# Row-by-row fetches by SyncE for 37 tiles of a graph network's gathers

## The reference

```python
h = relu(layernorm(x)); x = x + L0(h, edges)   # mean over neighbours, [h, mean] @ W.T + b
h = relu(layernorm(x)); x = x + L1(h, src, dst)
#   theta = h[dst] - h[src]; w = sigmoid(relu(theta @ W1 + b1) @ W2 + b2)
#   segment_sum(w * theta, dst) + indeg * (h @ W4 + b4)
h = relu(layernorm(x)); x = x + L2(h, edges)   # relu(h @ Wp.T + bp)[src], mean by dst, elu, normalised
h = relu(layernorm(x)); x = x + L3(h, ...)
#   all_h[etype, src] * edge_weight, segment_sum by dst, + h @ loop_weight
```

## Time and profile before

| | |
|---|---|
| Time, median of three runs | 5245.48 us (5244.3 to 5245.74) |
| Time of the profiled execution | 5255.77 us |
| Its span, first to last instruction | 5253.4 us |
| Mean granted TensorE clock | 0.846 of full speed |
| Busy: PE, DVE, ACT, POOL | 73%, 56%, 30%, 70% of the span |
| Gathers at line 1535 | 790 in layers 1 and 3, 1563 in layer 2, 1203 in layer 4 |
| DMA queue of SP and its packets | 145692 packets, 288.54 MB |

### The profile page before, as it was taken

One profiled execution on the slowest core, in us unless ns is written; L12 is line 12 of the kernel. 1 busy time (PEld: TensorE's weight loads), 2 busy tenths in 40 slices (PEclk: granted clock), 3 DMA queues, 4 the chain that ended last, 5 costly groups with the idle time before them and its releaser, 6 DMA issues.

```text
span 5253.4 us, 75208 instructions
## 1 busy us (share of the span) xinstructions
PE 3851.4 (73%) x22393; PEld 2977.7 (57%) x22393; DVE 2942.4 (56%) x9882; ACT 1575.8 (30%) x5791; POOL 3668.8 (70%) x3899
## 2 busy tenths in 40 slices
PE   3889999665666556566665488879899999999544
PEld 3345555655565555555555455445677777777443
DVE  7998876665555566666666744444544433333232
ACT  5555443433333333333333401132112222221000
POOL 5345553677777777777777477757777777777776
PEclk7799999877777777877778799989999999998655
DMA  4234443555555555555555556556111111111222
GB/s 124 69 123 141 145 145 125 166 156 158 157 157 157 157 156 158 159 159 158 159 161 161 153 191 201 200 178 244 52 50 51 51 51 50 51 51 52 53 73 53
DMA packets 303264, 663.89 MB, mean 126 GB/s; under 512 B 70592, under 2 KB 152924, under 8 KB 293388
## 3 DMA queue, kind: packets, MB, share of 16 engines
q0 software_dynamic: 155152, 369.61, 25.7%
q1 hardware_dynamic: 145692, 288.54, 16.3%
q10 hardware_dynamic: 2016, 0.92, 0.1%
HBM read 545.40 MB, written 113.38 MB: 125 GB/s over the span
## 4 chain that ended last, share of the span: by engine, by line
POOL 48%; PE 21%; issue 17%; DVE 9%; DMA 2%; ACT 2%; DVEq 1%; SPq 0%; ACTq 0%; POOLq 0%
POOL rows L1535 40%; POOL third L1535 8%; PE ps L2721 6%; PE ps L2618 3%; PE ps L2706 3%; PE ps L2630 2%; PE ps L2679 2%; DVE tmp L2019 2%; PE ps L2567 1%; PE ps L2686 1%; DVE oneh L1928 1%; DVE turned_words L2020 1%; DVE rows L2020 1%; DMA rows<-tab_hp,idx_src 1%; ACT h L1710 1%
## 5 line engine op out<-in xcount | busy, mean ns | idle before, releaser
L1535 POOL DMA_INDIRECT rows<-tab_rel,third x1203 | 1190.4, 990 | 366.7 <-issue 364.0
L1535 POOL DMA_INDIRECT rows<-tab_hp,idx_src x1120 | 1083.5, 967 | 345.2 <-issue 335.9
L2744 PE MATMUL ps<-third 128*128 128x128 f32 x3126 | 626.4, 363 | 729.4 <-DVE third L2049 728.7
L1535 POOL DMA_INDIRECT rows<-tab_h,idx_src x790 | 772.2, 977 | 541.2 <-PE ps L2686 276.2
L2744 PEld LDWEIGHTS ps<-third 128*128 128x128 f32 x3126 | 548.3, 264 | 790.5 <-DVE third L2049 789.5
L1758 ACT ACTIVATE turned_words<-turned_words 128x128 f32<-128x128 f32 x1563 | 463.2, 297 | 1251.0 <-DVE turned_words L2062 1251.0
L2721 PE MATMUL ps<-third,h 128*128 128x385 bf16 (+1 forms) x3626 | 742.7, 335 | 44.3 <-DMA h<-cnt_d 24.6
L2679 PE MATMUL ps<-oneh,rows 128*128 128x128 f32 x2406 | 403.2, 320 | 262.8 <-DMA rows<-tab_rel,third 160.1
L2679 PEld LDWEIGHTS ps<-oneh,rows 128*128 128x128 f32 x2406 | 352.5, 225 | 330.3 <-issue 183.2
L1535 POOL DMA_INDIRECT third<-tab_hp,idx_src x443 | 426.9, 964 | 135.0 <-issue 133.8
L2721 PEld LDWEIGHTS ps<-third,h 128*128 128x128 bf16 x3626 | 351.5, 100 | 293.8 <-issue 29.6
(11 more groups left out here) (305 smaller groups left out, 5685.6 us busy)
## 6 DMA issues: line engine op xcount, KB each, us to landing
third<-dst_flat SPq DMA_DIRECT2D x390, 256.0 KB, 3.5
cnt_d<-h SPq DMA_DIRECT2D x37, 1568.0 KB, 5.8
h<-cnt_d SPq DMA_DIRECT2D x37, 1568.0 KB
tab_rel<-third SPq DMA_DIRECT2D x49, 512.0 KB, 3.1
rows<-tab_rel,third POOLq DMA_INDIRECT x1203, 2.5
rows<-tab_hp,idx_src POOLq DMA_INDIRECT x1120
rows<-tab_h,idx_src POOLq DMA_INDIRECT x790
third<-tab_hp,idx_src POOLq DMA_INDIRECT x443
```

Source lines behind the costliest of these rows:

```text
L1535: pool.indirect_dma_start(out=to[:, t, 0:n], out_offset=None, in_=table[:, :], in_offset=bass.IndirectOffsetOnAxis(ap=idx[:, col:col + 1], ...
L2744: last = pe.matmul(ps_t[sl][:, t * P:(t + 1) * P], onehT[:, sl, t * P:(t + 1) * P], pwin[:, st["v"] % 2, :], start=True, stop=True)
```

## The change

In layer 2 the last tile of groups 20, 40, ..., 380 (19 tiles) and in layer 4 the last tile of groups 108, 124, ..., 380 (18 tiles) is no longer gathered by POOL. In each of the 16 turns that end two turns before the group's own, SP loads eight indices from one partition into registers and issues eight DMAs, each of one row, from the table to one partition of a buffer; there are two buffers a layer, in parts of `third` and of `key` that lie unused. In the group's turn SP waits until all 128 rows are there and the group's slot is free, and copies the buffer to the slot's last tile with one DMA. DVE's `hidden` and PE's `scatter` wait for this copy too. The indices come, one partition a tile, by 19 DMAs of 128 words at the start of layer 2, for which SP waits, and by 18 DMAs of one column of `parked` (128 words that lie apart) ahead of the loads of `late`.

```diff
--- before.py
+++ after.py
@@ -29,6 +29,8 @@
 BUNDLE = 128
 SPARE_COLS = 8
 OFF_LOAD = 8
+SINGLES = {1: (("sp", 20, 20),), 3: (("sp", 18, 16),)}
+ROW_LOAD = 8
 
 PACKS3 = ((4, 36, 2), (2, 76, 2), (1, 148, 2), (1, 244, 3))
 SLOTS3, NQ3 = 16, 3
@@ -226,7 +228,8 @@
         cut.append(cut[3] + (HP_SLOT - HP_FIRST) * hp_words)
         hT_early = third[:, cut[4]:cut[4] + CH * P]
         stage2_early = third[:, cut[4] + CH * P:cut[4] + 2 * CH * P].rearrange("p (b f) -> p b f", f=P)
-        assert cut[4] + 2 * CH * P <= nb * H3 // 2
+        cut.append(cut[4] + 3 * CH * P)
+        assert cut[5] + 4 * P <= nb * H3 // 2
         rows_hp = [v.rearrange("p (t f) -> p t f", f=2 * P + 1) for v in hp_at]
         dst_bc = third[:, cut[0]:cut[1]].rearrange("p (s e) -> p s e", s=3)
         onehT = third[:, cut[1]:cut[2]].rearrange("p (s e) -> p s e", s=2)
@@ -272,6 +275,11 @@
         key = sb("key", [P, npt])
 
         key3 = key[:, 0:nth]
+        single_at = {(1, "sp"): [third[:, cut[5] + k * 2 * P:cut[5] + (k + 1) * 2 * P] for k in range(2)]}
+        for n, who in enumerate(("sp", "act")):
+            single_at[3, who] = [key[:, CH * P + (2 * n + k) * P:CH * P + (2 * n + k + 1) * P] for k in range(2)]
+        idx_single = {1: key[:, 2 * CH * P:2 * CH * P + P].bitcast(I32), 3: key[:, 2 * CH * P:2 * CH * P + P].bitcast(I32)}
+        assert nth <= CH * P
         rest0 = key[:, 0:2 * CH * P].rearrange("p (s b f) -> p s b f", s=2, f=P)
         wsum = sb("wsum", [BUNDLE, P + 2])
         gsum = sb("gsum", [P, P + 2])
@@ -370,6 +378,9 @@
         s_wlo = sem("s_wlo")
         s_place = sem("s_place")
         s_off = sem("s_off")
+        s_rowidx = sem("s_rowidx")
+        s_moved = {(layer, who): [sem(f"s_moved{layer}{who}{k}") for k in range(2)] for layer in SINGLES for who, _, _ in SINGLES[layer]}
+        s_single = {(layer, who): [sem(f"s_single{layer}{who}{k}") for k in range(2)] for layer in SINGLES for who, _, _ in SINGLES[layer]}
         s_key3 = sem("s_key3")
         s_key3T = sem("s_key3T")
         s_idx3 = sem("s_idx3")
@@ -849,13 +860,32 @@
                 n_scat.update(n_scat_head)
                 added_before = s_add.value
             n_bc, n_pw, n_oneT, n_expand, n_hid, n_z, n_gate = ({} for _ in range(7))
+            singles, single_of, single_full, n_moved = {}, {}, {}, {}
+            for who, first, step in SINGLES.get(layer, ()):
+                singles[who] = list(range(g0 + first, ng - ROW_LOAD, step))
+                single_of.update((g, (who, j)) for j, g in enumerate(singles[who]))
+
+            def single_rows(g):
+                for who in singles:
+                    for j, at in enumerate(singles[who]):
+                        r0 = (g - (at - P // ROW_LOAD - 1)) * ROW_LOAD
+                        if 0 <= r0 < P:
+                            if r0 == 0:
+                                single_full[who, j] = s_single[layer, who][j % 2].up(16 * P)
+                            free = n_moved[singles[who][j - 2]] if j > 1 and r0 == 0 else None
+                            plan.append(("single_rows", dict(layer=layer, who=who, j=j, r0=r0, free=free)))
 
             def gather(g):
                 if g in n_row:
                     return
                 sl = g % slots
-                n_row[g] = s_row[sl].up(16 * tiles[g])
-                plan.append(("gather", dict(layer=layer, g=g, slot=sl, free=slot_free.get(sl))))
+                n_row[g] = s_row[sl].up(16 * (tiles[g] - (g in single_of)))
+                plan.append(("gather", dict(layer=layer, g=g, slot=sl, free=slot_free.get(sl), n=tiles[g] - (g in single_of))))
+                if g in single_of:
+                    who, j = single_of[g]
+                    n_moved[g] = s_moved[layer, who][j % 2], s_moved[layer, who][j % 2].up(16)
+                    plan.append(("single_copy", dict(layer=layer, who=who, j=j, slot=sl, t=tiles[g] - 1, free=slot_free.get(sl),
+                                                     full=single_full[who, j])))
 
             def onehot(g):
                 n_one[g] = s_one.up()
@@ -876,7 +906,8 @@
                     for _ in far_tails.pop(v - banks, ()):
                         pass
                 plan.append(("scatter", dict(layer=layer, g=g, v=v, slot=g % slots, sums=sums, one=n_one[g], row=n_row[g],
-                                             first=first, last=last, add=n_gadd.get(v - banks, added_before if layer == 3 else 0))))
+                                             first=first, last=last, add=n_gadd.get(v - banks, added_before if layer == 3 else 0),
+                                             moved=n_moved.get(g))))
                 if last:
                     far_tails[v] = (finish3 if layer == 3 else finish_far)(v, n_scat[g])
                     tails.append(far_tails[v])
@@ -1109,7 +1140,7 @@
 
             def hidden(g):
                 n_hid[g] = s_hid.up()
-                plan.append(("hidden", dict(g=g, slot=g % slots, expand=n_expand[g], row=n_row[g], diff=s_diff.up(),
+                plan.append(("hidden", dict(g=g, slot=g % slots, expand=n_expand[g], row=n_row[g], moved=n_moved.get(g), diff=s_diff.up(),
                                             z=n_z.get(g - 2, 0))))
 
             def gates(g):
@@ -1117,7 +1148,7 @@
                 plan.append(("gates", dict(g=g, hid=n_hid[g], z=n_z[g], gate=n_gate.get(g - 2, 0), one=n_one.get(g - 2, 0))))
 
             plan.append(("edges_begin", dict(layer=layer, tabh=s_tabh.value, tab=[s.value for s in s_tab], node=s_node.value,
-                                             relu=s_relu.value, hT=s_hT.value, mm=s_mm.value, h=s_h.value, sub=s_sub.value,
+                                             relu=s_relu.value, pack=s_pack.value, hT=s_hT.value, mm=s_mm.value, h=s_h.value, sub=s_sub.value,
                                              lo=s_lo.value)))
             if layer == 0:
                 for g in range(g0, min(g0 + H3_SLOT, ng)):
@@ -1158,6 +1189,7 @@
             dense3_left = layer == 3
             for turn in range(turns):
                 tails[:] = [tail for tail in tails if next(tail, "end") != "end"]
+                single_rows(g0 + turn)
                 for behind, step in steps:
                     if 0 <= turn - behind < ng - g0:
                         step(g0 + turn - behind)
@@ -1365,7 +1397,16 @@
                     last.then_inc(q["scat"], 1)
 
 
+        single_groups, row_at_single = {}, {}
+        for layer in SINGLES:
+            single_groups[layer] = []
+            for who, first, step in SINGLES[layer]:
+                row_at_single[layer, who] = len(single_groups[layer])
+                single_groups[layer] += range((0, 0, 0, HEAD_END)[layer] + first, ng - ROW_LOAD, step)
+        n_rowidx = 16 * sum(len(groups) for groups in single_groups.values())
+
         def sync_program(sp):
+            row_regs = [sp.alloc_register(f"row{k}") for k in range(ROW_LOAD)]
             sp.wait_ge(s_pad.handle, n_pad)
             for i, (c, m) in enumerate(chunks):
                 full = m - 1 if c + m == nb else m
@@ -1422,6 +1463,11 @@
                 elif kind == "late":
                     sp.wait_ge(s_pack.handle, st["pack"])
                     sp.wait_ge(s_park.handle, s_park.value)
+                    with nc.allow_non_contiguous_dma(reason="one index of each partition"):
+                        for k, g in enumerate(single_groups[3]):
+                            t = g * TPG + TPG - 1
+                            sp.dma_start(idx_single[3][k:k + 1, :].bitcast(U32), parked[0][:, t:t + 1].rearrange("p o -> o p")
+                                         ).then_inc(s_rowidx.handle, 16)
                     sp.dma_start(idx_rel, parked[0][:, :]).then_inc(s_late.handle, 16)
                     sp.dma_start(wt, parked[1][:, :]).then_inc(s_late.handle, 16)
                     sp.dma_start(wrel.rearrange("p (r o) -> p r o", r=n_rel),
@@ -1462,6 +1508,36 @@
                         sp.wait_ge(s_tab[k].handle, st["tab"][k])
                     sp.wait_ge(s_node.handle, st["node"])
                     sp.wait_ge(s_relu.handle, st["relu"])
+                    sp.wait_ge(s_pair.handle, s_pair.value)
+                    sp.wait_ge(s_pack.handle, st["pack"])
+                    for k, g in enumerate(single_groups[1]):
+                        t = g * TPG + TPG - 1
+                        sp.dma_start(idx_single[1][k:k + 1, :], ins["src"][t * P:(t + 1) * P].rearrange("(o e) -> o e", o=1)
+                                     ).then_inc(s_rowidx.handle, 16)
+                    sp.wait_ge(s_rowidx.handle, 16 * len(single_groups[1]))
+                elif kind == "edges_begin" and st["layer"] == 3:
+                    for k in range(3):
+                        if st["tab"][k]:
+                            sp.wait_ge(s_tab[k].handle, st["tab"][k])
+                    sp.wait_ge(s_rowidx.handle, n_rowidx)
+                elif kind == "single_rows" and st["who"] == "sp":
```

(23 more changed lines are left out.)

## The result

| | this | before, same batch | ratio, 95% interval |
|---|---|---|---|
| median | 5204.93 us (5203.18 to 5207.41, 4 runs) | 5245.61 us (5244.3 to 5247.63, 4 runs) | 0.9922 [0.9905, 0.9940] |

The change is faster by 40.7 us. The forecast was 5199.5 us, with a range of 5189 to 5300 and a chance of 0.69 on faster; the time is 5.4 us above it. The profiled execution after took 5203.18 us with a span of 5200.9. The one of before stood 10 us above its own median, so the two spans, 52.5 us apart, overstate the gain.

The account below looks back on a forecast made before the run. POOL's gathers were taken to bound layers 2 and 4. Gathers gone, -46.5 us, and late index DMAs, +0.5, sum to -46; the timed median of 5245.5 less 46 gives 5199.5 us, range 5189 to 5300.

Parts of the forecast that it names:

- Part 1: Layers 2 and 4: 37 gathers leave POOL, each with its gap; 46.2 to 47.4 us saved, taken as 46.5.
- Part 2: SP's row fetches in layers 2 and 4: 0.50 us a row, hidden in SP's waiting, so they cost nothing.
- the lag of 2 us in 16 turns: SP's turn in layer 4: 5.2 us against POOL's 5.1, a lag covered by three groups fetched ahead.
- The far bound: SP's row DMA: 0.59 us, upper end of the range, from line 1400's one-partition copies of 576 bytes.
- rival (c): SP becomes the bound in both layers: row DMA 0.59 us, r = 0.84, some 6380 us; chance 0.18.
- Part 3: Before layer 2: 19 index DMAs take SP 6 to 12 us, within 18.7 us of room; cost 0.
- Part 4: Between layers 3 and 4: 18 index DMAs ahead of the late loads, 6 to 12 us; cost 0 to 1 us.
- the list of signs: Trace signs; for PE's line 2567 behind the late loads' issue: right if still about 27 us, wrong if over 18.
- Part 5: DMA load: a tile's bytes stay, one copy is added, POOL doesn't wait for landings; 0 us.
- (a): PE becomes the bound in layer 4's dense part, 18 us of the gain lost, 5218 us; chance 0.06.
- (b): SP just misses, in layer 4 first: r = 0.60, 5264 us; chance 0.14, a part of it faster.
- both break-evens: Cost of one row up to which SP keeps POOL's pace: 0.61 us in layer 2, 0.55 in layer 4.

Follow-up runs that it names:

- pool_alone: The changed kernel without SP's rows and copies, the 37 gathers still left out; 5202.94 us, 44.2 less than the kernel before.
- only4: The changed kernel with single tiles in layer 4 only, layer 2 gathered as before; 5228.28 us, 18.9 less than the kernel before.
- sp_alone: The changed kernel with POOL gathering every tile, SP fetching rows unused, no copies or waits for them; 5247.76 us, +0.6 against before.
- dense12_b: The changed kernel with a single tile every 12 groups in both layers, index DMAs early; 5791.0 us, +544 against before.
- idx_early: The changed kernel with layer 4's index DMAs issued at the start; other chip 6332.98 us, ratio 1.0605 to before; repeated elsewhere 5197.80 us, ratio 0.9908.
- cut16: The changed kernel with each row's DMA written as 16 pieces, compiled to one piece again; 6322.63 us on the other chip, +353 against before.

## Why the prediction was right

**What bounds.** Right. POOL's gathers are the chain before and after, and pool_alone gives the whole gain without SP's rows and copies.

**Part 1, -46.5 us.** Right in total, and a little off in each layer. In layer 2 the four full traces with 19 tiles fewer (1957.4, 1953.0, 1955.1, 1954.0) have a mean of 1954.9, against 1979.9 for only4 and sp_alone with all tiles: -25.0, or 1.31 us a tile where 1.25 was taken. In layer 4 it is 1533.1 against 1555.0, -21.9 or 1.22 a tile. Together -46.9. The execution of before is left out in layer 2, where it stood at 1986.5; with it in, layer 2 gives 27.2 us, 1.43 a tile. Single traces of one layer stand 4 to 7 us apart, so neither figure is told from the 1.27 and 1.29 of the earlier trace rows.

**Part 2, cost 0.** Right: sp_alone measured +0.6 us. The DMA was put at 0.25 us by line 1387 and is 0.228, and the three short instructions at 0.10 to 0.30 and are 0.14 (0.419 less 0.228 and the gap of 0.05). The row is r = 0.42, not 0.50. The load of eight was mis-sized the other way: 0.73 us at the median, not ACT's 0.55. The two errors leave a turn at 4.60 us in place of 5.2, so the lag of 2 us in 16 turns doesn't arise. The far bound was line 1400's 0.59 us, which a row from memory didn't take; whether the pieces or the memory make line 1400 dearer wasn't tested. Part 2 calls the dear form "the second rival's"; by its 0.59 us it is rival (c).

**Part 3, cost 0.** Right. The 19 index DMAs take 0.25 us each, 5.6 us in all with the gaps, and the first scatter starts at 996.0 instead of 993.8, with POOL not waiting.

**Part 4, 0 to 1 us.** The issue time came out at its upper bound of 0.64 us: 0.64 each at the median (597 ns and a gap), 0.68 in the mean with one of 1.4, 12.3 us in all where 6 to 12 stood. The cost is put at about 1.5 us by the gaps, a little above. The 12 us went where the room was: from the end of layer 3's gathers to the last store of h it took 30.1 us before (3507.8 to 3537.9) and 31.0 after (3478.1 to 3509.1), the 13 stores spread over 13.8 us in place of 25.1. PE's line 2567 (now 2645) starts at 3508.7, 13.9 us behind the issue of the last late load instead of 27.

```profile
L1473 SPq DMA_DIRECT2D third<-in_L_gnn_weight x1: 433/433/433, 3494.8 to 3494.8; - x1
...
L1482 SPq DMA_DIRECT2D tab_pb<-h x13: 548/855/3110, 3495.3 to 3509.1; - x13
```

This is what Part 4 implies (27 less the 12 us that the loads are later). But the list of signs has it otherwise: it asks for "still about 27 us" if right and over 18 if wrong, which can't both be. The first was a slip, and it did not come true.

**Part 5, 0.** Right: POOL's mean gather is unchanged (963 and 988 ns), and so it is in sp_alone.

**The sum.** -46.9 + 1.5 = -45.4 us from the stretches, -43.1 to -43.6 from the paired kernels, -40.7 as timed, with an interval of 31 to 50 us. The 5.4 us between the forecast and the time lie within that interval, so no step needs to have failed for them. That the terms' small errors partly cancel (the row dear, the load cheap) was luck, but it didn't decide: both were in SP's hidden time.

**The rivals.** (a) fell: POOL waits 5.8 us for scatters in layer 4 after 2.7 before, and layer 4 gives 1.22 us a tile, dense part included. (b) and (c) fell at the price of a row: 0.42, below both break-evens. Their mechanism is real: dense12_b reaches it with more rows a turn, the other chip with slower rows, and in both the symptoms are those written down (SP's waits all but gone, DVE on the window fetch, POOL on slots). The chance of 0.18 on (c) was for a dearer DMA form; a chip whose sequencers pause was not among the causes considered.

## What to carry over

Where one engine's queue is the bound and another's waits for most of the time, moving a few work items across is worth about what the item cost the bound engine, here 1.2 to 1.3 us a tile, as long as the receiver's cost of one item times their rate stays below the bound's pace; compute that ratio for each stage, since it is a cliff and not a slope (a tile every 16 groups in layer 2 still gained, one every 12 lost 544 us). Price a DMA first by the row that has the same direction, memory and number of contiguous pieces: that one gave 0.25 us for 0.228 measured, the one nearest in bytes 0.59. And keep margin: a program that issues 14,880 more small instructions depends on what an engine's queue takes for one, and on one chip of those used here a row took nearly twice as much (0.78 us for 0.43).

## What the runs showed of the hardware

A DMA of one contiguous row of 512 or 1024 bytes to one partition issues in 0.225 to 0.228 us on SP and 0.224 on ACT, no more than 256 bytes did, while 128 words of four bytes in one DMA take 0.60. Loading eight register words takes SP 0.73 us at the median, against 0.267 for one. On one chip, SP's row DMAs were recorded at 1 to 1407 ns where they took 224 to 308 on the others, the kernel before took 14 per cent longer, and the change turned from 0.8 per cent faster into 6 per cent slower (measured there with idx_early and cut16, whose rows on SP are those of the change).
